# A loop over expert tiles: four row and result buffers, four tiles a turn, turned rows in halves, and earlier base adds

## The reference

```python
probs = jax.nn.softmax(xt @ W_router, axis=-1)
top_v, top_i = jax.lax.top_k(probs, K_TOP)
gate = jnp.sum(jax.nn.one_hot(top_i, E_rt, dtype=xt.dtype) * top_v[..., None], axis=1)
rt_mid = jax.nn.gelu(jnp.einsum('th,ehd->ted', xt, Wrt_up), approximate=False)
routed_out = jnp.einsum('ted,edh->th', rt_mid * gate[:, :, None], Wrt_down)
return (shared_out + routed_out).reshape(B, S, H)
```

## Time and profile before

| | us |
|---|---|
| time, median of 3 runs | 926.66 (924.68 to 927.26) |
| time of the profiled execution | 921.43 |
| its span in the trace | 919.7 |
| PE busy | 887.2 (96% of the span) |
| DVE busy | 502.7 (55%) |
| ACT busy | 402.0 (44%) |
| POOL busy | 384.2 (42%) |

### The profile page before, as it was taken

The page is one execution under the profiler, slowest core; times in us unless marked ns, Lnnn a source line. Parts: engine busy times, 40 slices in busy tenths (PEclk is TensorE's granted clock), DMA queues, the critical chain, the costliest instruction groups (busy, mean ns, idle before and its releaser), DMA issues.

```text
span 919.7 us, 13596 instructions
## 1 busy us (share of the span) xinstructions
PE 887.2 (96%) x4264; PEld 715.2 (78%) x4265; DVE 502.7 (55%) x967; ACT 402.0 (44%) x688; POOL 384.2 (42%) x282
## 2 busy tenths in 40 slices
PE   6899989999998999999999999999999999999996
PEld 2367778788776888888888888888887887888875
DVE  4685999884847111454135513651496444444388
ACT  3575875875645432322232223225444333333352
POOL 3231120100022546226202530258537699998473
PEclk9899999999999999999999999999999999999998
DMA  9659577654155328396214321466435788775787
GB/s 357 218 176 307 167 244 253 204 185 135 49 189 201 114 92 274 119 288 212 92 34 158 118 92 35 154 218 212 161 115 195 244 255 264 271 272 207 250 248 192
DMA packets 122401, 174.07 MB, mean 189 GB/s; under 512 B 8792, under 2 KB 70232, under 8 KB 119280
## 3 DMA queue, kind: packets, MB, share of 16 engines
q1 hardware_dynamic: 59472, 111.58, 35.5%
q0 software_dynamic: 9216, 34.61, 12.1%
q10 hardware_dynamic: 53664, 27.26, 10.3%
HBM read 97.60 MB, written 75.83 MB: 189 GB/s over the span
## 4 chain that ended last, share of the span: by engine, by line
PE 84%; ACT 5%; DMA 4%; DVE 3%; issue 2%; POOL 1%; SPq 0%; ACTq 0%; DVEq 0%
PE kk_ps L427 6%; PE kv_ps L427 6%; PE kk_ps L429 6%; PE kv_ps L429 6%; PE kk_ps L428 6%; PE kv_ps L428 6%; PE mm_ps L427 6%; PE mm_ps L428 6%; PE mm_ps L429 6%; PE up_ps L427 4%; PE dn_ps L427 3%; PE dn_ps L429 3%; PE dn_ps L428 3%; PE up_ps L428 3%; PE up_ps L429 3%
## 5 line engine op out<-in xcount | busy, mean ns | idle before, releaser
L1576 DVE TENSOR_TENSOR silu<-kk_ps,silu 128x512 fp32r<-128x512 f32 x64 | 44.3, 691 | 199.9 <-ACT silu L2266 199.6
L2262 ACT ACTIVATE kk_ps<-kk_ps 128x512 f32<-128x512 f32 x64 | 37.2, 582 | 206.8 <-PE kk_ps L429 206.8
L427 PE MATMUL kk_ps<-xk,cm_w 128*128 128x512 f32 x256 | 100.9, 394 | 0.0
L427 PE MATMUL kv_ps<-cm_w,silu 128*128 128x512 f32 x256 | 100.5, 393 | 0.0
L429 PE MATMUL kk_ps<-xk,cm_w 128*128 128x512 f32 x256 | 99.8, 390 | 0.0
L429 PE MATMUL kv_ps<-cm_w,silu 128*128 128x512 f32 x256 | 99.7, 390 | 0.0
L428 PE MATMUL kk_ps<-xk,cm_w 128*128 128x512 f32 x256 | 99.6, 389 | 0.0
L428 PE MATMUL kv_ps<-cm_w,silu 128*128 128x512 f32 x256 | 99.6, 389 | 0.0
L2439 POOL TENSOR_TENSOR rs<-mv,neghalf 128x4 f32<-128x4 f32 (+2 forms) x13 | 15.8, 1217 | 152.6 <-DVE mv L1327 139.9
L2432 POOL TENSOR_TENSOR cm_w<-stage,cm_w 128x1024 fp32r<-128x1024 f32 x16 | 38.7, 2422 | 91.1 <-ACT cm_w L2026 72.3
L2490 POOL TENSOR_TENSOR rs<-mv,neghalf 128x1 f32<-128x1 f32 x16 | 16.1, 1008 | 127.4 <-DVE mv L1601 127.4
(11 more groups left out here) (306 smaller groups left out, 2345.9 us busy)
## 6 DMA issues: line engine op xcount, KB each, us to landing
xs_s<-zero ACTq DMA_DIRECT2D x13, 1024.0 KB, 7.9
ys_s<-zero ACTq DMA_DIRECT2D x13, 1024.0 KB, 6.3
xsb<-xs_s SPq DMA_DIRECT2D x44, 256.0 KB, 3.7
ys_s<-ysb SPq DMA_DIRECT2D x41, 256.0 KB, 4.1
ex_raw<-in_wex POOLq DMA_DIRECT2D x9, 1024.0 KB, 6.7
stage<-in_wcm SPq DMA_DIRECT2D x16, 512.0 KB, 3.7
wmod<-in_wmod SPq DMA_DIRECT2D x6, 1024.0 KB, 11.7
ex_raw<-in_wex SPq DMA_DIRECT2D x6, 1024.0 KB, 7.2
```

The costliest lines, as they stand in the source:

```text
L427: pe.matmul(out, lhs[0], rhs[0], start=first, stop=False)
L1576: dve.tensor_tensor(silu[:, g % NSILU, 1, :], kk_ps[g % 2][:, :], silu[:, g % NSILU, 0, :].bitcast(F32), ALU.subtract).then_inc(s_silo, 1)
L2262: act.activation(kk_ps[g % 2][:, :], kk_ps[g % 2][:, :], ACT.Silu).then_inc(s_silu, 1)
```

## The change

Six things change, most of them in the loop over the tiles.

1. Loaded rows have four buffers (`xsb` and a new `xsb2`), and results four (`ysb`, and the buffer `stage`, which is free by then). Tile q uses the slot q mod 4, with semaphores that are used again from earlier stages (`XS_BASE`, `YS_BASE` are their counts so far).
2. The loops on PE, DVE, ACT and SP run over four tiles a turn (`quad`), ten turns instead of twenty, for the same 41 tiles.
3. The turned rows of a tile lie half in either PSUM bank: the blocks 0 and 1 in the one, 2 and 3 in the other. PE announces each half, ACT and DVE each work on two 128x256 halves instead of one 128x512, and `up` waits for the second half only before its seventh matmul.
4. Ahead of the loop, the second tile is turned after nine matmuls of the shared expert and not before them, and two more tiles (4 and 5) are loaded. SP doesn't load in its last turn.
5. POOL's eight `base_add` move from between the experts 5 to 8 to the loop's entry, and the loads of the experts 5 and 6 move by one place. The split of an expert announces itself with its last instruction and doesn't wait for it any more.
6. Ahead of its first gather, POOL waits for four result slots, one after another, instead of two.

```diff
-            def load_xs(q, par, wait=None):
+            def load_xs(q, s, turned=None):
                 tile = tile_of(q)
-                if wait is not None:
-                    sp.wait_ge(s_tx, wait)
-                sp.dma_start(xsb[:, par], rows(xs_s, tile)).then_inc(s_xs[par], 16)
+                if turned is not None:
+                    sp.wait_ge(s_tx, turned * 2)
+                sp.dma_start(xs_rows(s), rows(xs_s, tile)).then_inc(s_xs[s], 16)
...
+            sp.wait_ge(s_dn, SB * TT)
+            load_xs(4, 2)
+            load_xs(5, 3)
             load_ht(NB - 1)
...
+            def quad(i, loads):
+                for k in range(4):
+                    if loads:
+                        load_xs(i * 4 + 6 + k, k, i * 4 + 3 + k)
+                    store_y(i * 4 + k, k, i * 4 + 1 + k + AHEAD)
...
-            def turn_x(par, xs_count):
-
-                pe.wait_ge(s_xs[par], xs_count)
+            def turn_x(par, s, xs_count):
+
+                pe.wait_ge(s_xs[s], xs_count + XS_BASE[s])
                 for k in range(KT):
-                    mm = pe.transpose(xs_ps[par][:, k, :], xsb[:, par, k * P:(k + 1) * P], ident[:, :])
-                mm.then_inc(s_tx, 1)
+                    mm = pe.transpose(xs_ps[k // 2][:, par * 2 + k % 2, :], xs_rows(s)[:, k * P:(k + 1) * P],
+                                      ident[:, :])
+                    if k % 2:
+                        mm.then_inc(s_tx, 1)
...
                 pe.wait_ge(s_exr, word)
-                pe.wait_ge(s_txlo, count)
                 for k in range(KT):
+                    if k % 2 == 0:
+                        pe.wait_ge(s_txlo, count * 2 - 1 + k // 2)
...
-            turn_x(0, 16)
-            turn_x(1, 16)
+            turn_x(0, 0, 16)
             shared_down(1, [3], first)
+            pe.wait_ge(s_txlo, 2)
+            turn_x(1, 1, 16)
             pe.wait_ge(s_gsh, SB * TT - 2)
             up(w0, slot_of(w0), 0, 1)
...
+            def quad(i, w0, w1):
+                for k in range(4):
+                    up(w1, slot_of(w1), (k + 1) % 2, i * 4 + k + 2)
+                    turn_x(k % 2, k, i * 16 + (32 if k < 2 else 16))
+                    down(slot_of(w0), k % 2, i * 4 + k + 1, i * 4 + k + 1)
+                    w0, w1 = w1, word_of(i * 4 + k + 2)
+                    turn_m((k + 1) % 2, i * 4 + k + 2)
+                return w0, w1
...
             def turned_lo(par, count):
-                dve.wait_ge(s_txhi, count)
-                dve.tensor_tensor(xsT[:, par, 1], xs_ps[par][:, :, :], xsT[:, par, 0].bitcast(F32), ALU.subtract)\
-                    .then_inc(s_txlo, 1)
+                for h in range(2):
+                    dve.wait_ge(s_txhi, count * 2 - 1 + h)
+                    dve.tensor_tensor(xsT[:, par, 1, h * 2:h * 2 + 2], xs_ps[h][:, par * 2:par * 2 + 2, :],
+                                      xsT[:, par, 0, h * 2:h * 2 + 2].bitcast(F32), ALU.subtract).then_inc(s_txlo, 1)
...
             def turned_hi(par, count):
-                act.wait_ge(s_tx, count)
-                act.activation(xsT[:, par, 0], xs_ps[par][:, :, :], ACT.Copy).then_inc(s_txhi, 1)
+                for h in range(2):
+                    act.wait_ge(s_tx, count * 2 - 1 + h)
+                    act.activation(xsT[:, par, 0, h * 2:h * 2 + 2], xs_ps[h][:, par * 2:par * 2 + 2, :], ACT.Copy)\
+                        .then_inc(s_txhi, 1)
...
-                n = 2 * (e - PRE)
+                n = e - PRE
                 pool.tensor_tensor(hi, raw_of(e), zero[:, 0:1].to_broadcast([P, UNIT]), ALU.add).then_inc(s_exd, 1)
                 pool.wait_ge(s_exd, n + 1)
-                pool.tensor_tensor(lo, raw_of(e), hi.bitcast(F32), ALU.subtract).then_inc(s_exd, 1)
-                pool.wait_ge(s_exd, n + 2)
-                pool.sem_inc(s_exr, 8)
+                pool.tensor_tensor(lo, raw_of(e), hi.bitcast(F32), ALU.subtract).then_inc(s_exr, 8)
...
+            for t in range(TT):
+                base_add(t)
             pool.wait_ge(s_tab, 1)
             for par in range(2):
                 pool.wait_ge(s_xs[par], 16)
             expert_load(PRE)
             ht_lo(2)
+            for t in range(TT, SB * TT):
+                base_add(t)
+            expert_load(PRE + 1)
             expert_split(PRE)
-            expert_load(PRE + 1)
 
             for e in range(PRE + 1, NE):
-                if e + 1 < NE:
+                if PRE + 1 < e < NE - 1:
                     expert_load(e + 1)
                 expert_split(e)
-                if e <= PRE + TT:
-                    base_add(2 * (e - PRE - 1))
-                    base_add(2 * (e - PRE - 1) + 1)
+                if e == PRE + 1:
+                    expert_load(e + 1)
...
-            for i in range(2):
-                stored = pool.value_load(tend[0:1, NE + 1 + i:NE + 2 + i], min_val=16, max_val=16 * NS + 16)
+            for i in range(4):
+                stored = pool.value_load(tend[0:1, NE + 1 + i:NE + 2 + i], min_val=YS_BASE, max_val=4 * NS + 16 + YS_BASE)
                 pool.wait_ge(s_yst[i], stored)
```

More of the change, by code:

```diff
@@ L1909, in turned_mid_lo, with y_out @@
                     .then_inc(s_tmlo, 1)
-            def y_out(par, count, stored):
+            def y_out(s, count, stored):
                 dve.wait_ge(s_d4, count)
-                if stored is not None:
-                    dve.wait_ge(s_yst[par], stored)
-                dve.tensor_copy(ysb[:, par], dn4_ps[par][:, :]).then_inc(s_y4, 1)
-            dve.sem_inc(s_yst[1], 16)
-            dve.sem_inc(s_yst[0], 16)
+                dve.wait_ge(s_yst[s], stored)
+                dve.tensor_copy(ys_rows(s), dn4_ps[s % 2][:, :]).then_inc(s_y4, 1)
+            dve.sem_inc(s_yst[1], YS_BASE)
+            dve.sem_inc(s_yst[0], YS_BASE)
             turned_lo(0, 1)
@@ L1925, in _ @@
             turned_mid_lo(0, 1)
-            pairs = dve.value_load(tend[0:1, NE:NE + 1], min_val=NE // 2, max_val=NS // 2)
-            def pair(i):
-                turned_lo(0, i * 2 + 3)
-                y_out(0, i * 2 + 1, i * 16 + 16)
-                turned_mid_lo(1, i * 2 + 2)
-                turned_lo(1, i * 2 + 4)
-                y_out(1, i * 2 + 2, i * 16 + 16)
-                turned_mid_lo(0, i * 2 + 3)
-            with dve.Fori(0, pairs) as i:
-                pair(i)
-            y_out(0, pairs * 2 + 1, pairs * 16 + 16)
+            quads = dve.value_load(tend[0:1, NE:NE + 1], min_val=NE // 4 - 1, max_val=NS // 4 - 1) + 1
+            pairs = quads * 2
+            with dve.Fori(0, quads) as i:
+                for k in range(4):
+                    turned_lo(k % 2, i * 4 + k + 3)
+                    y_out(k, i * 4 + k + 1, i * 16 + YS_BASE)
+                    turned_mid_lo((k + 1) % 2, i * 4 + k + 2)
+            y_out(0, pairs * 2 + 1, pairs * 8 + YS_BASE)
             def upper_row(t):
@@ L2363, in _ @@
             act.wait_ge(s_tab, 1)
[L2364 to L2371 removed]
+            quads = act.value_load(tend[0:1, NE:NE + 1], min_val=NE // 4 - 1, max_val=NS // 4 - 1) + 1
+            with act.Fori(0, quads) as i:
+                for k in range(4):
+                    gelu4((k + 1) % 2, i * 4 + k + 2)
+                    turned_hi(k % 2, i * 4 + k + 3)
+                    turned_mid_hi((k + 1) % 2, i * 4 + k + 2)
             def scaled(tiles):
```

85 lines of the change are left out of this document (35 added, 50 removed).

## The result

The changed kernel takes 931.25 us in the median of 20 runs (927.74 to 934.23), the kernel before 927.27 (924.68 to 932.93). The ratio is 1.0036, 95% interval [1.0023, 1.0049]: slower by 0.4%, where 0.8% faster (918.9) was forecast. Its profiled execution took 932.1 us and has a span of 930.3, 10.6 more than the 919.7 of before.

The account below looks back on a forecast made before the run. The prediction took a ring of waits through ACT and DVE to bound the loop. Its terms, 7.1 + 2.6 - 0.4 - 1.5 = 7.8 us gained at the first gather, took the median of 926.66 to 918.9, range 915 to 923.5.

Parts of the forecast that it names:

- Ring and halves: Loop: waits from PE through ACT and DVE set 3.73 us a tile; half rows save 0.23, giving 3.50.
- Branch tile: Loop: of four tiles a turn, the one behind the branch gains only 0.08 us, the other three 0.23 each.
- more than that: Loop and gather: branch hidden and wait rounds costing 0.5 us in all; gain 10.2, time 916.5; chance 0.14.
- Four buffers: Loop: all 2.6 us of stalls on loads and stores go; lower bound 1.3.
- Table load: Loop entry: ACT loads the gelu's table later, so the gelu and PE's next step come 0.4 us later.
- POOL: Loop: expert 13 ready at 820.5, 1.7 us to spare; as rival, POOL becomes the bound: 920.9 to 923.9, chance 0.11.
- Gather waits: Ahead of the first gather: two more rounds of waiting on POOL cost 0.75 us each, 1.5 in all.
- First gather: Behind the loop: POOL's first gather starts near 852, a gain of 7.8 us.
- DVE's tail follows at the same distance: Behind the loop: DVE's combining keeps its distance to the first gather, so the 7.8 us gained there reach the end.
- Against the median of before: Whole kernel: the profiled execution was 5.2 us below the median, so the gain was taken from the median of 926.66.
- PE's instruction stream: Loop: PE's own instructions are the next bound, a tile gains 0.08 us, time 923.0; chance 0.14.
- The loop body isn't fetched again: Loop: the rival had PE's longer body fetched again each turn, 1.1 to 1.6 us, time 930 to 935; chance 0.07.

Follow-up runs that it names:

- again: The changed kernel, unaltered, timed once more in two runs: 917.14 us, ratio 0.9927 to the kernel before.
- again_b: The changed kernel, unaltered, timed a third time: 929.78 us, ratio 1.0019 to the kernel before.
- again_c: The changed kernel, unaltered, timed again as yardstick for its variants: 934.65 us, ratio 1.0073 to the kernel before.
- old_split: The changed kernel, but POOL again waits for a split's end before announcing it: 940.47 us.
- gather_late: The changed kernel with six more rounds of small steps on POOL, so that its first gather starts 3.5 us later: 925.66 us.
- plain_gather: The changed kernel with the first ten gathers as plain copies of as many bytes: 914.09 us, ratio 0.9856 to the kernel before.
- after_plain: The changed kernel with the first ten gathers as plain copies, as in plain_gather, timed again: 913.72 us, ratio 0.9824 to the kernel before.
- old_pool: The changed kernel with POOL as before (base adds, order of expert loads, wait behind a split): 923.36 us, ratio 0.9981 to the kernel before.
- before_c: The kernel before, unaltered, run once more for a trace of its own: 928.32 us.
- comparison A: One chip's runs of again, the halves alone, old_pool and whole rows, beside the kernel before, whose median there was 925.1 us.
- before_late: The kernel before with its first gather 3.5 us later: 941.08 us, ratio 1.0138 to the kernel before.
- base_end: The changed kernel with the second four base adds moved to POOL's idle time ahead of the gathers: 919.91 us, ratio 0.9909 to the kernel before.
- base_end_b: The same program as base_end, timed again: 922.33 us, ratio 0.9946 to the kernel before.

## Why the prediction was wrong, point by point

- **Ring and halves: right.** 3.50 a tile was forecast, 3.48 measured. PEld's idle time ahead of `up` is gone (0.6 us in `again`), and back with whole rows.
- **Branch tile: a little better.** I let it gain 0.08, from one sample; the chain shows all tiles 3.48 apart but two, 3.67 (at 745.88) and 3.61. The rival "more than that" was right in this.
- **Four buffers: right, its lower bound in one of two ways.** No load stalls the loop behind its entry. The entry stall came in the profiled execution (a load of 11.95 us) with 3.8 us and in `again` with 2.9, against my bound of 1.3. Six other traces with the same entry (`again_b`, `again_c`, `old_split`, `gather_late`, `plain_gather`, `after_plain`) have 0 to 0.6.
- **Table load: 0.4 was too much.** The gelu came at 711.17 instead of 711.03, 0.14 later.
- **POOL: right.** Expert 13 was ready at 815.79 + 4.62 = 820.4 (forecast 820.5). Its rounds are 9.05 us without the 0.74 idle, so the read of the word hides. `old_split` and `old_pool` show how near the bound is: without the early announcement the expert comes 6 us late.
- **Gather waits: 1.2 and not 1.5.** Two rounds of 0.57 and 0.59.
- **First gather: 853.69 and not 852**, by the entry stall. Without part of it, in `again`, 852.16: 7.6 us gained at the first gather, where the sum said 7.8.
- **"DVE's tail follows at the same distance": this is the step that failed.** The first combining step did follow, 16.44 us behind the first gather (16.57 before). Behind it I took 43.4 us as given. It was 60.2. I had read DVE as the bound behind the loop and never asked what feeds it there: PE's results, announced to ACT while the gathers run. As a term of the sum it was 0, and it is +16.8 in the profiled execution. In `again` without late announcements it is still +3.5, where three of POOL's gathers take 2.8 to 3.4 us each, and DVE then waits 4.8 for one. Only with plain copies in both kernels is it the same in both.
- **Against the median of before: a second slip of the same kind.** I moved the profiled 921.43 up by 5.2 to the median and asked nothing about those 5.2. `before_c`, with a span 4.9 longer than that of before, shows what they are in good part: the kernel before has late announcements itself, and they bring its first gelu behind the loop 5.5 us later. The changed kernel has three of them. So the trace of before, with 10,459 records and no lateness, showed nothing of what its own median held.
- **The rivals.** PE's instruction stream isn't the bound (3.48), POOL isn't. The loop body isn't fetched again. The page's part on queues for the changed kernel:

```profile
q8 instruction: 28, 0.46, 0.2%
```

  One packet more than in the earlier trace rows, for 129 instructions more, and not one a turn. The Trainium skill, "Runtime: NRT & Kernel Launch", "Instruction fetch mechanics", has a store of two blocks, in which a taken branch to a block that has gone stalls for a fetch, and in the same place gives PE a larger store. The trace doesn't agree with the two blocks for PE but does with the larger store: one packet came between 720 and 725, in the loop's first two turns, and then none until behind the loop, so the block with the loop's head wasn't fetched again in the eight turns that followed. The time of that case, 930 to 935, came for another reason; that the number fits is chance.

So the mechanism of the loop on which the forecast rested was right: 7.6 us at the first gather in `again`, and 10.9 of gain in the pair with plain copies. That `again` took 917.1 is in part luck, since its trace gives 3.5 of the 7.6 back behind the loop, and two runs stand for it. The forecast of the measured median was wrong by a cost behind the loop that I had at nothing.

**What stays open** is why PE's results are announced late. Shown is that it goes with the ten gathering DMAs (plain copies of the same size, issued faster, don't bring it), that both kernels have it, that its size changes with their start, and that all of comparison A goes without it. Every trace with the loss lacks records of semaphore updates. So do those with plain copies, which have no loss, so the missing records tell of the surroundings and not of the cause. The Trainium skill, "NOTIFIC — the notification-queue block", section "Overflow: three behaviours, one of which stalls the engine", names among what a full queue of records does that records are lost, and that an engine is held up. No run here can show whether either happens. That the fourth gelu of `before_late` is caught and those of `base_end` aren't (in `base_end_b`, the same program, ACT waits 1.5 us for the fourth), I can't explain.

## What to carry to other kernels

When the loop ahead of a tail gets shorter, the tail is not carried along as it is: list what is awaited in it and ask for each wait which transfer now runs beside it. Take parts that remove different bounds together, or they measure as nothing: here one or two of three parts gave at most 2 us, and all three 8 to 11. And a version should be timed in more than one comparison where a single program has given 917 and 935; a pair of variants with the suspect taken out of both tells more than many repeats.

## What the runs showed of the hardware

While POOL's gathering DMAs ran, results of PE reached ACT 2 to 21 us behind PE's rows in at least eight traces, of either kernel, and on time in others; beside plain DMAs with as many bytes, at up to 342 GB/s, none was late in three traces. Three gathers of `again` took POOL longer to issue (timeline of POOL):

```profile
876.75 2.77 POOL L2608 DMA_INDIRECT g1b<-ys_s,spos  x1 [0.31 <-issue]
879.82 3.43 POOL L2608 DMA_INDIRECT g1b<-ys_s,spos  x1 [0.30 <-issue]
883.55 3.43 POOL L2608 DMA_INDIRECT g1b<-ys_s,spos  x1 [0.30 <-issue]
```

Most others take 0.96. At that time DVE combines with two inputs from SBUF without a gap; the Trainium skill, "GPSIMD Engine Reference", "Specifications", says that the two share their way to SBUF for such steps. The traces don't bear it out as the cause here, since in the kernel before DVE does the same steps just as densely beside gathers of 0.96 (window with the columns of the earlier trace rows, then POOL, trace of before):

```profile
885.00:895.00 10.00, 9.57 (x43) 7.61 (x41) 10.00 (x17) 2.53 (x5) 6.84 (x8) 1.00 0.89 276
```
```profile
885.94 0.95 POOL L2595 DMA_INDIRECT g1b<-ys_s,spos  x1 [0.30 <-issue]
887.20 0.96 POOL L2595 DMA_INDIRECT g1b<-ys_s,spos  x1 [0.31 <-issue]
```

Why those three are longer stays open. And a load of 128 rows, 3.9 us in the median of `again`, took 12.9 at worst, at the entry, where eight adding transfers and two loads of 1 MB of weights are issued within 18 us.
